# Moving the loads and the centring of the expert weights inside the blocks of a fused attention and expert kernel

## The reference

```
x = x + xattn(layernorm(x), ctx)          # 16 heads, 77 context rows, then relu(out @ W1 + b1) @ W2 + b2
x = x + moe(layernorm(x))                 # top-1 of 8 experts
  top1 = argmax(xt @ Wg.T)
  xhat = (xt - mu) * rsqrt(var + eps)
  h    = gelu((xhat * s_e + b_e) @ w1_e + bb1_e)      # 512 -> 128
  y    = h @ w2_e + bb2_e  for the tokens with top1 == e
```

## Time and profile before

| | |
|---|---|
| median of 3 runs | 1382.98 us (1382.66 to 1385.61) |
| the profiled execution | 1382.66 us, span in the trace 1380.9 us |
| granted TensorE clock, mean | 0.999 |
| PE busy | 1358.1 us (98%) |
| DVE busy | 1000.4 us (72%) |
| ACT busy | 609.0 us (44%) |
| POOL busy | 338.0 us (24%) |

### The profile page before, as it was taken

The page is one execution under the profiler, slowest core; times in us unless marked ns, Lnnn a source line. Parts: engine busy times, 40 slices in busy tenths (PEclk is TensorE's granted clock), DMA queues, the critical chain, the costliest instruction groups (busy, mean ns, idle before and its releaser), DMA issues.

```text
span 1380.9 us, 23796 instructions
## 1 busy us (share of the span) xinstructions
PE 1358.1 (98%) x8366; PEld 1015.2 (74%) x8366; DVE 1000.4 (72%) x2129; ACT 609.0 (44%) x1146; POOL 338.0 (24%) x293
## 2 busy tenths in 40 slices
PE   7999999999999999999999999999999999999997
PEld 5486868677776768686868677776868686788996
DVE  6777677687778777777878677867676767558666
ACT  4434334443434343534344343524343433357885
POOL 2311211103020212121120202021212121128886
PEclk9999999999999999999999999999999999999999
DMA  7200302213040404131231303040303032559884
GB/s 297 76 29 3 93 31 67 88 36 123 22 139 9 138 24 117 50 101 61 63 99 31 123 25 114 6 122 1 117 7 106 18 92 76 189 170 302 285 260 140
DMA packets 66998, 132.85 MB, mean 96 GB/s; under 512 B 11241, under 2 KB 19698, under 8 KB 65986
## 3 DMA queue, kind: packets, MB, share of 16 engines
q1 hardware_dynamic: 56082, 97.63, 23.5%
q0 software_dynamic: 10800, 33.70, 6.4%
HBM read 73.77 MB, written 44.66 MB: 86 GB/s over the span
## 4 chain that ended last, share of the span: by engine, by line
PE 94%; DVE 2%; issue 1%; DMA 1%; POOL 1%; ACT 0%; another core or an unknown queue 0%; SPq 0%; POOLq 0%; ACTq 0%; DVEq 0%
PE bank L1221 25%; PE bank L1265 13%; PE bank L1245 12%; PE bank L1054 12%; PE bank L1144 8%; PE bank L1126 5%; PE bank L1647 4%; PE bank L1685 3%; PE bank L1079 2%; PE bank L1307 2%; PE bank L1631 2%; PE bank L1325 1%; PE bank L1098 1%; PE bank L898 1%; DMA region<-rows,pos 0%
## 5 line engine op out<-in xcount | busy, mean ns | idle before, releaser
L1221 PE MATMUL bank<-actA,w 128*128 128x512 f32 x1536 | 368.6, 395 | 1.4 <-DVE actA L1192 1.4
L1221 PEld LDWEIGHTS bank<-actA,w 128*128 128x128 f32 x1536 | 282.4, 188 | 63.4 <-issue 5.6
L1134 ACT ACTIVATE E<-bank 77x512 f32<-77x512 f32 x256 | 132.5, 592 | 172.8 <-PE bank L1126 172.7
L1265 PE MATMUL bank<-w,actH 128*128 128x512 f32 x768 | 195.7, 400 | 0.0
L1396 POOL DMA_INDIRECT region<-rows,pos x64 | 66.5, 1039 | 487.0 <-DVE rows L1296 451.6
L1054 PE MATMUL bank<-actA,wq 128*128 128x512 f32 x768 | 182.7, 390 | 0.0
L1245 PE MATMUL bank<-w,actH 128*128 128x512 f32 x768 | 179.6, 391 | 0.0
L1092 DVE TENSOR_REDUCE mx<-bank 128x4 f32<-128x308 f32 x256 | 104.8, 473 | 95.0 <-PE bank L1079 94.9
L1265 PEld LDWEIGHTS bank<-w,actH 128*128 128x128 f32 x768 | 138.7, 188 | 44.6 <-issue 18.3
L1245 PEld LDWEIGHTS bank<-w,actH 128*128 128x128 f32 x768 | 143.4, 188 | 29.5
L1054 PEld LDWEIGHTS bank<-actA,wq 128*128 128x128 f32 x768 | 142.7, 188 | 28.2 <-issue 0.5
(11 more groups left out here) (182 smaller groups left out, 1831.2 us busy)
## 6 DMA issues: line engine op xcount, KB each, us to landing
rowB<-region SPq DMA_DIRECT2D x71, 258.0 KB
xn<-in_x SPq DMA_DIRECT2D x64, 256.0 KB
rows<-in_x SPq DMA_DIRECT2D x64, 256.0 KB, 3.4
xn<-xq SPq DMA_DIRECT2D x224, 64.0 KB, 2.0
w_raw<-in_W SPq DMA_DIRECT2D x2, 2048.0 KB, 11.8
e_raw<-in_E SPq DMA_DIRECT2D x16, 256.0 KB, 3.4
region<-padrow SPq DMA_DIRECT2D x9, 258.0 KB, 2.3
e_parts<-e_high SPq DMA_DIRECT2D x8, 256.0 KB, 2.5
```

Source lines behind the costliest of these rows:

```text
L1134: act.activation(E[0:M, g % 2, h, :], of("ST", b, g, h)[0:M, :], ACT.Exp).then_inc(S["act_exp"], 1)
L1221: mm = pe.matmul(p[:], w, a, start=k == 0 and j == 0, stop=k == KD - 1 and j == 2)
L1265: mm = pe.matmul(p[:], actH[:, ha, m, P * s:P * s + P], w2[:, hw, m, :], start=n == 0, stop=n == 23)
```

## The change

Only the list of steps is changed. In blocks 3 to 10, `XNLOAD(b+1, 2)` and `XNLOAD(b+1, 0)` now stand at the start of the H phase, as in all other blocks; they stood in the tail of the block before, around `E2_STORE`. `E1_RAW` now comes directly behind `E2_RAW` in the tail, ahead of `E2_STORE`. `E1_SUM` goes from the second half of `Y(b,1)` up to the H phase, behind `H(b,6)` and ahead of `RK`; `E1_CENTER` and `E1_STORE` follow it at m = 6.

```diff
-            elif not PREP0 < b <= PREP0 + NE:
+            else:
                 step("XNLOAD", b + 1, 2)
                 step("XNLOAD", b + 1, 0)
...
                 step("HHI", b, m)
+                if prep is not None and m == 6:
+                    step("E1_SUM", prep)
...
                         if prep is not None:
                             step("E1_ACC", prep)
+                if prep is not None and m == 6:
+                    step("E1_CENTER", prep)
+                    step("E1_STORE", prep)
...
                 step("YA", b, 1)
-                if centre is not None:
-                    step("E1_SUM", centre)
                 for s in range(2, SUB):
                     step("XTS" if b + 1 >= DT else "XT", b + 1, s)
-                if centre is not None:
-                    step("E1_CENTER", centre)
-                    step("E1_STORE", centre)
                 if prep is not None:
                     step("E2_RAW", prep)
-                    step("XNLOAD", b + 2, 2)
+                    step("E1_RAW", prep)
...
                 if prep is not None:
                     step("E2_LOW", prep)
                     step("E2_STORE", prep)
-                    step("XNLOAD", b + 2, 0)
-                    step("E1_RAW", prep)
```

More of the change, by code:

```diff
@@ L477, in xattn_moe_kernel @@
             else:
-                centre = prep
                 prep = b - PREP0 if PREP0 <= b < PREP0 + NE else None
```

## The result

The changed kernel takes 1440.02 us (median of 4 runs, 1438.69 to 1441.93) against 1383.7 for the kernel before (median of 4 as well): a ratio of 1.0407, with a 95% interval of 1.0389 to 1.0424. That is 56 us slower where 9.6 were forecast. The direction and the place were right, the size was not. The profiled execution has a span of 1437.7 us, 56.8 more than before.

What follows compares the result with a forecast made beforehand. PE, without slack, was taken to bound the kernel: E1_SUM's waits +11.2 us, less 1.6 regained in the tail, give +9.6 on a median of 1382.98, so 1392.6 us; range for 8 in 10, 1388.5 to 1399.5.

Steps and rivals of the forecast that it cites:

- E1_SUM behind H(b,6): H phase, blocks 3 to 10: PE waits for E1_ACC, 1.4 us in each of eight blocks, 11.2 us.
- the low end of 11.0: E1_SUM's wait over eight blocks if its weight load stays hidden: 11.0 us; the high end, load open, 12.5.
- Token loads: cost nothing: H phase: xn[0] lands 3.4 us after issue, hidden by 1.5 us; cost nothing, ends 0 and 8 us.
- The rival of the late token loads: xn[0] lands over 7.4 us after issue, six transfers at once; one microsecond beyond slack costs 8: 1400.6 us; 8%.
- The clock: Rival: 36 matmuls per block at 1.2 instead of 2.4 GHz, 65 us over eight blocks, 1458 us; 2%.
- The two rivals: Token loads too late, 1400.6 us, 8%; and the clock falls in each block, 1458 us, 2%.
- E1_CENTER on DVE, E1_STORE, the tail: E1_CENTER at m = 6 costs nothing; E2_RAW issued without the store and token loads beside it gains 1.6 us.
- The wait on `mx`: Sign: PE's waits on mx vanish and ACT's wait for e_raw falls below 30.4 us.
- the excess of blocks 6 and 9: Blocks 6 and 9 last 0.62 and 1.11 us longer than block 5; 1.73 us together, the most to win.

Runs made afterwards that it cites:

- the run with plain rows: Changed kernel, token tiles of blocks 2 and up loaded as 128 rows in a row, without regrouping (output not the reference's): 1392.27 us, ratio 1.005.
- the run whose clock was held: Changed kernel with 18 useless matmuls ahead of E1_SUM's wait in each of eight blocks: 1416.17 us, ratio 1.0223.
- the moved sum alone: Kernel before with only E1_SUM, E1_CENTER and E1_STORE moved to m = 6, all loads on SP as before: 1392.91 us, ratio 1.0057.
- the run with the moved loads alone: Kernel before with E1_RAW behind E2_RAW and token loads in the H phase, E1_SUM still in the tail: 1403.5 us, ratio 1.0124.
- The lone move of `E2_RAW`: Kernel before with only E2_RAW moved ahead of the loads of the block rows on SP: 1380.96 us, ratio 0.9964.
- the run with the stores first: Changed kernel with E2_STORE ahead of E1_RAW on SP: 1397.23 us, ratio 1.0082.

## Why the prediction was wrong, step by step

**E1_SUM behind H(b,6), 1.37 us in each block.** Right, shown by itself: 10.9 us in eight waits, the low end of 11.0, so no weight load stands open. The Trainium skill ("TensorE: Matmul & The Clock Gate", "Step-by-step: what each phase is for") has weight loads pulled ahead of running matmuls; the low end agrees with that.

**Token loads: cost nothing.** This is the step that failed, by one number, and it brought on the failure of the next one: "`xn[0]` is issued there and lands 3.4 us later, as the row loads do". The row loads move the same 256 KB, but from 128 rows in a row. The token loads read four groups of 32 rows. The trace of before had the real rate in it. Its DMA activity from 630.3 to 644, when only the last two token loads of the tail run, in 40 slices:

```profile
DMA  0000402122222222222221000100000000000000
GB/s 0 0 0 0 48 18 60 48 90 108 102 96 114 102 96 96 114 102 96 102 102 42 24 0 0 48 0 0 0 0 0 0 0 0 0 0 0 0 0 0
```

The share stands at two tenths and the rate at some 100 GB/s for five microseconds: 512 KB / 100 GB/s = 5.2 us for the pair, 10.5 us for all four, where I had counted on a fixed 3.4 us each. The bytes end about 637.8, more than 7 us after the issue of the first of the pair at 630.38. In the changed kernel the same shows while the four run:

```profile
688.00:690.00 2.00, 2.00 (x12) 1.65 (x11) 1.90 (x2) 0.04 (x1) 0.00 (x0) 1.00 0.25 96
```

0.25 is what 4 of 16 engines that are always busy would give; the profile does not name the engines. The Trainium skill has the rule ("DMA: Bandwidth & Descriptors", "Why a DMA increments its semaphore by 16 and not by 1"): the number of engines of a copy is the largest one up to 16 that divides the slowest dimension of both sides, here 4. By that rule the trace agrees, with its share of 0.25, and so do the runs with plain rows and with four DMAs for each tile.

The rest of that step held in kind. I had written that DVE could catch up by at least 2.5 us and that lateness beyond it would reach `E1_ACC` one to one. DVE waited (57.8 - 5) / 8 = 6.6 us. Measured from the end of the scores, `E1_ACC` ended 713.53 - 682.05 = 31.48 us later in block 8, and 674.73 - 646.33 = 28.40 before, by this line:

```profile
674.38 0.35 DVE L1412 SCALAR_TENSOR_TENSOR e_acc<-e_raw,lns,e_acc 128x128 f32<-128x128 f32 x1
```

So DVE caught up 3.5 of the 6.6 us, 1 us more than my count, and 3.1 us were left: 1.37 + 3.1 = 4.5 us is PE's wait. The rival of the late token loads, 8%, named this path, its place and its price of 8 us for one; its reason, six transfers at once, was not the right one, as the run with plain rows shows. With 3.1 us it would have given 1392.6 + 25 = 1417, near the 1416.17 of the run whose clock was held.

**The clock.** A rival with 2%, and it came true in part. My reason against it was one wait of 1.4 us in the trace of before, behind which the clock stayed. It was sound for waits of 1.4 us (the moved sum alone: 0.999) and said nothing on 4.5. I had priced whole groups of 36 matmuls at the lower level, 65 us; it was the stretch from 713.68 to 720.20, 21.4 us in eight blocks. The sum now closes: eight waits of 36.3 us and 21.4 us of slower work are 57.7, and the span is 56.8 longer; the forecast had 11.2 us of this, the other 46.5 are the late loads, 25 us, and the clock behind them. The Trainium skill's section on a kernel whose idles between matmul groups make the clock swing ("TensorE: Matmul & The Clock Gate", "A second HAM failure mode: psum-queue depth-cycling") was dismissed too soon: that idles on PE lower the clock is what the traces now show, at 0.51 granted behind the wait of 4.45 us in block 8, and in the run with the moved loads alone behind four waits of 1.78 to 2.62 us. The two rivals were counted as exclusive, while one brings on the other.

**E1_CENTER on DVE, E1_STORE, the tail.** Right in direction. The wait on `mx` is gone, ACT's wait fell from 30.4 to 19.8 us. The lone move of `E2_RAW` shows that the excess of blocks 6 and 9 came from there. The size stays open: in the run of the moved sum alone the waits are 10.9 us and the span is 10.2 longer, so 0.7 us came back where I had put 1.6; by the medians, with 7.4 us, it would be more, and the stages behind the blocks vary by as much.

## What to carry to other kernels

A load that is hidden now has no price in the page; before it is moved to where it is waited for, read its rate from the DMA share and the GB/s while it runs alone. Here the bytes alone did not tell it: 256 KB landed in 3.4 us or in over 9, by the shape of the source. On this PE without slack, each wait of over 4 us was paid twice, once standing (4.5 us) and once at half clock (2.7 us), so price the two together, and a queue of DMAs behind a semaphore that comes late is the first place to look for such a wait.

## What was not expected of the hardware

- The same 256 KB took 3.4 us from plain rows and over 9 us as the third of four regrouped loads, at 0.25 of the engines and about 100 GB/s; as four DMAs of 64 KB each part landed in 1.9 us.
- 18 matmuls of no use in each of eight blocks made the changed kernel 1.8% faster, by keeping the granted clock at 1.00.
- In the run with the moved loads alone, four of eight waits of PE ended in slow matmuls, and not by length alone: behind one of 1.90 us the twelve matmuls of H(b,7) took 4.57 us, behind one of 2.04 us 3.00. In the run with the stores first it fell behind a wait of 2.29 us and not behind one of 2.27. The waits of 1.37 us in the run with the moved sum never cost the clock, those of over 4 us in the changed kernel did so each time.
